# One decoder layer on one core: the dispatch step of the experts stage in another order, with work moved between engines, and merged weight loads

## The chip, the cores and the metric

One core of one Trainium2 chip runs the whole program in one launch. A core has TensorE (PE in the rows), VectorE (DVE), ScalarE (ACT), GpSimd (POOL) and SyncE (SP, here only an issuer of DMAs). The metric is the device time in microseconds (us), lower is better.

## The reference

The input `x` is 128 sequences of 64 tokens of 128 numbers. Three residual blocks follow one another:

```
x = x + attn(layernorm(x))            # 128 positions attend per token column: softmax(tanh(q k)), values are the input
x = x + xattn(layernorm(x), ctx)      # 16 heads of 8
x = x + ffn(layernorm(x))             # soft mixture of 16 experts with 16 slots each
# ffn, for each sequence b of 64 tokens n, with xn = layernorm(x)*gamma + beta
logits   = (xn/|xn| * scale) @ (mu/|mu|)           # n x 256 slots
dispatch = softmax(logits over n); combine = softmax(logits over the 256 slots)
slot_in  = dispatch^T @ xn                         # 256 slots x 128
slot_out = gelu(slot_in @ w1 + b1) @ w2 + b2       # per expert, hidden 32
out      = combine @ slot_out
```

## The kernel before

The program is hand-written per engine: each engine has its own stream of instructions, in the order in which it stands in the code, and semaphores between them. There are four parts, one after the other. All are loops over 16 chunks of 512 tokens, software-pipelined: in step `t` an engine works on chunk `t` in one phase, on chunk `t+1` in an earlier phase, and so on.

1. `self_attention` (first 93 us). SP first issues eight chunks of `x`, then the list `loads` (36 DMAs of weights, L174), four context chunks (L177), and only then goes on with one more chunk of `x` (L171) and one result chunk `x1` out (L181) per step. DVE normalises each chunk (`xn`, L233, four pieces of 128x128 of a chunk), ACT makes `yT`, `xT`, `th`, `pr`. `x1` has two buffers, so the `x1` of chunk 2 (L253) waits until that of chunk 0 has landed in DRAM.
2. `cross_attention`, which the change leaves alone.
3. `experts_in`, the dispatch part. For a chunk: statistics (DVE L1013, L1035), the power -0.5 of the variance (POOL, four ops ending with L956), normalised tokens `hat` (DVE L1025), `xn` = gamma and beta (POOL L963, L965), squares `junk` (ACT L1097), their sum and clamp (DVE L1008, L1019), the power -0.5 of it and times `scale` (POOL `rn`, L941, L943), unit tokens `xu` (DVE L1047), transposed `xuT` (PE L1161, ACT L1077), the logits in both layouts, transposed (PE L1125, called lT here) and not (PE L1131, lA). From them maxima `cm` and `rm` (DVE L1000, L1003), which PE turns into rows (L1140, L1141, here mT), ACT negates (`neg`, L1066), and PE adds back onto the logits as a shift by products with 0/1 matrices `pick` and `sel` (L1149, L1153). ACT takes the exponentials `comb` (L1071) and `disp` (L1083). In the next step PE gathers `slot_in` in two halves (L1115, here g0 and g1), both through the same two PSUM banks, so that g1 waits until ACT has copied the half of g0 (`e_slot_in`, L1057); then come the hidden layer (L1169), the sums of `disp` (L1177) and their copy `raw` (ACT L1091). The sums go through DRAM (SP L915 to L927, with waits in between) to the reciprocal `inv` (DVE L1041) and back to `rden`, and POOL makes `scaled` and `hidden` from them (L981, L984).
4. `experts_out`, which runs in the same block behind it: second layer and combination (PE L1286, L1300), with `comb` of each chunk loaded back from DRAM (SP L1206).

## Time and profile before

| what | us |
|---|---|
| median of 3 runs (lowest, highest) | 626.12 (625.14, 627.65) |
| the profiled execution, and its span | 625.29, 623.5 |
| self attention, 0 to 93.18: PE busy, DVE busy | 64.19, 58.36 |
| cross attention, 93.18 to 326.64: PE busy, DVE busy | 210.57, 179.21 |
| dispatch, start, 326.64 to 371.50: PE, POOL | 20.34, 31.31 |
| dispatch, 13 equal steps, 371.50 to 504.51: PE, POOL | 123.60, 88.47 |
| dispatch, end, 504.51 to 536.93: PE | 21.02 |
| experts out, 536.93 to 623.50: PE | 80.33 |

The kernel's time is 1.8 us more than the span, which runs from the first to the last recorded instruction. Where the PE is busy for all but some per cent of a stretch, the question is what its order of work costs; where it is not, who it waits for. A row of the timeline names the start, the duration, the engine and line, the operation with output and inputs, how many were merged into the row, and in square brackets how long the engine was idle before it and who ended that.

### The profile page before, as it was taken

To read this page: it belongs to the slowest core of one execution; us is meant where nothing else is said; L and a number is where in the kernel's file an instruction comes from. 1 tells how busy PE (TensorE), PEld (TensorE's weight loads), DVE (VectorE), ACT (ScalarE), POOL (GpSimd) and SP (SyncE) were. 2 spreads that over 40 slices of the span, in tenths; PEclk is the share of its full clock that TensorE was granted. 3 is DMA by queue.
4 is the path that set the end of the run, shared out by engine and by line. 5 is a ranking of instruction groups with operands and counts; after the bars stand their busy time and mean duration, and the time that the engine had idled before them with its cause. 6 is when DMAs were issued, how large, how long until landed. Compare 5 with 4: busy or idle time off the path is not lost. (4 is left out here: it accounts for less than half of the span.)

```text
span 623.5 us, 19720 instructions
## 1 busy us (share of the span) xinstructions
PE 520.1 (83%) x7660; PEld 371.6 (60%) x7660; DVE 410.1 (66%) x1187; ACT 345.1 (55%) x487; POOL 286.9 (46%) x369
## 2 busy tenths in 40 slices
PE   4748867989889999999860599999999983999996
PEld 3536655555356666666640355655555552999995
...
GB/s 181 87 178 120 76 58 129 165 137 44 2 22 38 26 36 39 31 30 40 38 20 1 0 70 54 90 68 88 72 100 59 103 56 71 132 152 150 150 149 100
DMA packets 60912, 49.30 MB, mean 79 GB/s; under 512 B 15648, under 2 KB 50592, under 8 KB 60832
## 3 DMA queue, kind: packets, MB, share of 16 engines
...
## 5 line engine op out<-in xcount | busy, mean ns | idle before, releaser
L567 DVE TENSOR_REDUCE c_mx<-ps 128x16 f32<-128x1024 f32 x64 | 78.0, 1218 | 12.9 <-PE ps L722 12.9
L521 POOL TENSOR_TENSOR c_k_bd<-c_k,w_mask 128x512 bf16<-128x512 f32 x80 | 83.7, 1071 | 1.2 <-DVE c_work L605 1.2
L1286 PE MATMUL ps<-w_w,h_bd 128*64 128x128 f32 x1024 | 71.5, 279 | 6.3 <-DVE o_slot_out L1238 6.3
L644 ACT ACTIVATE c_work<-ps 128x2048 f32<-128x2048 f32 x32 | 60.0, 1874 | 26.8 <-PE ps L751 26.8
L1286 PEld LDWEIGHTS ps<-w_w,h_bd 128*64 128x64 f32 x1024 | 63.2, 141 | 7.2 <-DVE o_slot_out L1238 7.2
L1230 ACT ACTIVATE h_bd<-hidden 32x512 f32 (+1 forms) x64 | 40.2, 628 | 41.4 <-PE ps L1286 40.8
L1057 ACT ACTIVATE e_slot_in<-ps 128x1024 f32<-128x1024 f32 x32 | 32.8, 1024 | 51.8 <-PE ps L1115 51.8
L1262 DVE TENSOR_TENSOR o_slot_out<-ps,w_b 128x512 f32<-128x512 f32 x64 | 44.0, 687 | 20.7 <-PE ps L1286 20.3
L1000 DVE TENSOR_REDUCE e_cm<-ps 128x16 f32<-128x1024 f32 x16 | 19.6, 1225 | 49.8 <-PE ps L1125 49.8
L1115 PE MATMUL ps<-e_disp,e_xn 64*128 64x256 f32 x256 | 36.3, 400 | 9.5 <-ACT e_slot_in L1057 8.3
L654 ACT ACTIVATE c_q_bd<-x_all,w_mask 128x512 f32<-128x512 f32 x64 | 42.8, 719 | 0.0
L1300 PE MATMUL ps<-o_slot_out,ctx_sb 128*64 128x129 f32 x512 | 41.9, 274 | 1.0 <-DMA ctx_sb<-combine_scratch 1.0
L1125 PE MATMUL ps<-e_xuT,w_mu 128*128 128x512 f32 x64 | 34.8, 669 | 4.5 <-ACT e_xuT L1077 4.5
L541 POOL COPY c_v_bd<-c_v 64x512 f32<-64x512 f32 x32 | 21.8, 681 | 35.8 <-PE ps L771 27.2
L751 PE MATMUL ps<-c_q_bd,c_k 32*64 32x256 f32 x1024 | 35.5, 375 | 0.4 <-issue 0.4
L771 PE MATMUL ps<-c_work,c_v_bd 128*18 128x64 f32 x2048 | 35.7, 223 | 0.0
L981 POOL TENSOR_TENSOR e_scaled<-e_raw,e_rden 128x512 f32<-128x512 f32 x16 | 20.3, 1270 | 32.3 <-DMA e_rden<-dispatch_inverses 32.3
L1115 PEld LDWEIGHTS ps<-e_disp,e_xn 64*128 64x128 f32 x256 | 23.3, 186 | 19.9 <-issue 19.3
L941 POOL TENSOR_TENSOR e_rn<-e_sq,w_neg_half 128x4 f32<-128x4 f32 x16 | 16.7, 1041 | 39.2 <-DVE e_sq L1019 39.1
L771 PEld LDWEIGHTS ps<-c_work,c_v_bd 128*18 128x18 f32 x2048 | 30.0, 99 | 7.5 <-issue 7.5
L1300 PEld LDWEIGHTS ps<-o_slot_out,ctx_sb 128*64 128x64 f32 x512 | 33.2, 137 | 1.5 <-DMA ctx_sb<-combine_scratch 1.5
L1097 ACT ACTIVATE e_junk<-e_xn 128x512 f32<-128x512 f32 x16 | 10.1, 630 | 43.1 <-POOL e_xn L965 43.1
...
## 6 DMA issues: line engine op xcount, KB each, us to landing
x_all<-x_scratch SPq DMA_DIRECT2D x128, 64.0 KB, 2.3
...
```

What stands on the lines that cost most here:

```text
L521: ins = nc.gpsimd.tensor_tensor(k_bd[:, c.m2, s, :], k32[:, c.v, :], w["mask8"][:, s:s + 1].to_broadcast([P, TOK]), ALU.mult)
L567: nc.vector.reduce_max(mx[:, c.m2, :, p], ps[:, SCORE:SCORE + 2, :].rearrange("p a (h m) -> p (a h) m", m=N), AX_X).then_inc(mx_sb.sem, 1)
L644: nc.scalar.activation(prob[:, h, :], ps[:, 0:4, :].rearrange("p a b -> p (a b)"), ACT.Exp, scale=float(HD) ** -0.5).then_inc(p_sb.sem, 1)
L654: ins = nc.scalar.activation(q_bd[:, c.m2, j, :], q32[:, c.v, :], ACT.Copy, scale=w["mask4"][:, j:j + 1])
L751: ins = nc.tensor.matmul(ps[N * r:N * (r + 1), T, a * 4 * N:(a + 1) * 4 * N].rearrange("p (j n) -> p j n", j=4), k32[rows, c.v, k_at:k_at ...
L771: ins = nc.tensor.matmul(ps[32 * j:32 * j + 2 * V1, VALUE, to:to + N], v_bd[:, c.m2, 2 * u + a, 4 * T + j, :], prob[:, u, of:of + N], star ...
L1115: ins = nc.tensor.matmul(ps[:, 6 + r, a * ES:(a + 1) * ES], xn[at, c.m4, 2 * h + a, :], disp[at, c.m2, 2 * h + a, :], start=True, stop=True)
L1125: ins = nc.tensor.matmul(ps[:, 3 + h, :], w["mu"][:, h * P:(h + 1) * P], xuT[:, c.m2, :], start=True, stop=False, skip_group_check=True)
L1230: ins = nc.scalar.activation(h_bd[at, c.m2, :, :, e, :].rearrange("p s g k -> p g s k"), hidden[at, :, bass.ts(c.v, SC * SLOTS)].rearrange ...
L1262: nc.vector.tensor_tensor(slot_out[:, c.m2, 2 * p:2 * p + 2, :, 0:D], ps[:, p, :].rearrange("p (s a d) -> p s a d", s=2, a=2), w["b2"][:]. ...
L1286: ins = nc.tensor.matmul(ps[64 * (g % 2):64 * (g % 2) + 64, p, at:at + D], h_bd[:, c.m2, s % 2 * PC + s // 2, g].rearrange("p e k -> p (e ...
L1300: ins = nc.tensor.matmul(ps[N * r:N * (r + 1), 4 + p // 2, (p % 2) * (D + 1):(p % 2 + 1) * (D + 1)], comb[:, c.m2, h, s * N:(s + 1) * N], ...
```

## The change

Self attention: of the four pieces of `xn` of a chunk DVE makes two and ACT the other two, as `Identity` with a per-partition scale and a per-partition bias `shift` = -mean times the root; POOL makes `shift` with two more small ops. Loads: `w2` comes in one DMA (before: four), `b2` in eight (before: sixteen), so 25 in place of 36. Dispatch part: `hat` is made by ACT in four pieces in the same way (POOL makes its `shift` with two more small ops), `neg` by DVE, the two powers of -0.5 are one POOL op over eight columns, the factor `scale` is folded into `mu` once, `xu` is one DVE op. The maxima and the identity that turns them are bf16; mT writes them to four groups of partitions (0, 32, 64, 96), and `pick` and `sel` stand in those groups, so that the products of the shift go to different row tiles of PE. The memsets of `sel32` and `pick32` and their affine selects are gone; `pick` and `sel` are made by DVE from the identity. The phases move: `scaled` and `hidden` one step later, `xn` by one step later relative to `hat`, and PE's order within a step is another.

PE, one steady step of `experts_in`, before (L1125 lT, L1131 lA, L1115 the gathers, L1140 and L1141 mT, L1149 and L1153 the shift, L1161 the transposes of `xu`):

```order
L1125 MATMUL ps<-e_xuT,w_mu 128x512 x2
L1131 MATMUL ps<-w_mu,e_xuT 128x256 x4
L1115 MATMUL ps<-e_disp,e_xn 128x256 x4
L1140 MATMUL ps<-w_ident,e_cm 8x128 x2
L1141 MATMUL ps<-w_ident,e_rm 8x128
L1115 MATMUL ps<-e_disp,e_xn 128x256 x4
L1149 MATMUL ps<-e_neg,e_pick 128x128 x8
L1153 MATMUL ps<-e_neg,e_sel 128x256 x4
L1161 MATMUL ps<-w_ident,e_xu 128x128 x4
L1169 MATMUL ps<-e_slot_in,w_w 32x128 x16
L1177 MATMUL ps<-e_disp,w_ones 32x256 x8
```

The same step now, up to the hidden layer, whose two rows stay as they were:

```order
L1164 MATMUL ps<-e_xuT,w_mu 128x512 x2
L1153 MATMUL ps<-e_disp,e_xn 128x256 x4
L1172 MATMUL ps<-w_mu,e_xuT 128x256 x4
L1153 MATMUL ps<-e_disp,e_xn 128x256 x4
L1182 MATMUL ps<-e_ident,e_cm 8x128 x4
L1185 MATMUL ps<-e_ident,e_rm 8x128 x2
L1192 MATMUL ps<-w_ident,e_xu 128x128 x4
L1200 MATMUL ps<-e_neg,e_pick 128x128 x2
L1204 MATMUL ps<-e_neg,e_sel 128x256
L1200 MATMUL ps<-e_neg,e_pick 128x128 x2
L1204 MATMUL ps<-e_neg,e_sel 128x256
```

The gather g0 has moved ahead of lA, so that lA stands between the two gathers; mT comes after g1; the transposes of `xu` have moved between mT and the shift; and the shift is interleaved (the last two rows come twice more).

ACT, one steady step of `experts_in`, before:

```order
L1057 ACTIVATE e_slot_in<-ps 128x2x2x256
L1066 ACTIVATE e_neg<-ps 8x384
L1057 ACTIVATE e_slot_in<-ps 128x2x2x256
L1071 ACTIVATE e_comb<-ps 128x1024
L1077 ACTIVATE e_xuT<-ps 128x512
L1083 ACTIVATE e_disp<-ps 128x1024
L1091 ACTIVATE e_raw<-ps 128x1024
L1097 ACTIVATE e_junk<-e_xn 128x512
```

And now:

```order
L1100 ACTIVATE e_hat<-x_all,e_shift,e_inv_root 128x128 x4
L1091 ACTIVATE e_slot_in<-ps 128x2x2x256
L1108 ACTIVATE e_junk<-e_xn 128x512
L1091 ACTIVATE e_slot_in<-ps 128x2x2x256
L1114 ACTIVATE e_xuT<-ps 128x512
L1119 ACTIVATE e_comb<-ps 128x1024
L1126 ACTIVATE e_disp<-ps 128x1024
L1134 ACTIVATE e_raw<-ps 128x1024
```

The `neg` has gone and four pieces of `hat` have come in at the head of the step; `junk` stands between the two slot copies, and `xuT` ahead of `comb`.

SP, the end of the list of loads in `self_attention`, before and now:

```order
L174 DMA w_w<-in_L_ffn_w 128x128
L174 DMA w_b<-in_L_ffn_b 128x1
L174 DMA w_w<-in_L_ffn_w 128x128
L174 DMA w_b<-in_L_ffn_b 16x128 x16
L177 DMA ctx_sb<-in_ctx 128x4x128 x4
```

```order
L176 DMA w_b<-in_L_ffn_b 128x1 x4
L176 DMA w_w<-in_L_ffn_w 128x4x128
L176 DMA w_b<-in_L_ffn_b 16x2x128 x8
L179 DMA ctx_sb<-in_ctx 128x4x128 x4
```

Eleven DMAs fewer stand ahead of the context chunks, and behind those come the result chunks.

```diff
+                    if c.plus(-2): pool.wait_ge(normed_act.sem, normed_act.at(c.plus(-2)))
                     nc.gpsimd.tensor_tensor(rstd[:, c.m2, :], mv[:, c.m2, :, 1], w["ln_eps"][:], ALU.add).then_inc(rooted.sem, 1)
-                    pool.wait_ge(rooted.sem, rooted.at(c, 1))
+                    nc.gpsimd.tensor_tensor(shift[:, c.m2, :], mv[:, c.m2, :, 0], neg_one[:], ALU.mult).then_inc(rooted.sem, 1)
+                    pool.wait_ge(rooted.sem, rooted.at(c, 2))
                     nc.gpsimd.tensor_tensor(rstd[:, c.m2, :], rstd[:, c.m2, :], w["neg_half"][:, 0:BC],
                                             ALU.pow).then_inc(rooted.sem, 1)
+                    pool.wait_ge(rooted.sem, rooted.at(c, 3))
+                    nc.gpsimd.tensor_tensor(shift[:, c.m2, :], shift[:, c.m2, :], rstd[:, c.m2, :], ALU.mult).then_inc(rooted.sem, 1)
...
-                    for b in range(BC):
+                    for b in range(BC // 2):
                         ins = nc.vector.tensor_scalar(xn[:, c.m4, b, 0:D], xc[:, b, :], mv[:, c.m2, b, 0:1],
                                                       rstd[:, c.m2, b:b + 1], ALU.subtract, ALU.mult)
...
+                c = t.plus(2)
+                if c:
+                    act.wait_ge(rooted.sem, rooted.at(c))
+                    if c.plus(-4): act.wait_ge(o_ps.sem, o_ps.at(c.plus(-4)))
+                    for b in range(BC // 2, BC):
+                        ins = nc.scalar.activation(xn[:, c.m4, b, 0:D], x_sb[:, bass.ds(c.v * BC + b, 1), :].rearrange("p a d -> p (a d)"),
+                                                   ACT.Identity, bias=shift[:, c.m2, b:b + 1], scale=rstd[:, c.m2, b:b + 1])
+                    ins.then_inc(normed_act.sem, 1)
...
+                    pe.wait_ge(normed_act.sem, normed_act.at(c))
...
-        loads.append((w["w2"][:, g, :], a["L0_ffn_w2"][4 * g:4 * g + 4].rearrange("c h d -> (c h) d")))
-    for e in range(EXPERTS):
-        loads.append((w["b2"][SLOTS * (e % 8):SLOTS * (e % 8 + 1), e // 8, :],
-                      a["L0_ffn_b2"][e:e + 1, :].to_broadcast([SLOTS, D])))
+    loads.append((w["w2"][:], a["L0_ffn_w2"].rearrange("(g c) h d -> (c h) g d", g=4)))
+    for e in range(8):
+        loads.append((w["b2"][SLOTS * e:SLOTS * (e + 1), :, :],
+                      a["L0_ffn_b2"].rearrange("(a e) d -> e a d", a=2)[e:e + 1].to_broadcast([SLOTS, 2, D])))
...
         for t in steps:
             c = t.plus(3)
             if c:
-                pool.wait_ge(clamped.sem, clamped.at(c))
-                if c.plus(-2): pool.wait_ge(xu_sb.sem, xu_sb.at(c.plus(-2)))
-                nc.gpsimd.tensor_tensor(rn[:, c.m2], sq[:, c.m2], w["neg_half"][:, 0:PC], ALU.pow).then_inc(unit.sem, 1)
-                pool.wait_ge(unit.sem, unit.at(c, 1))
-                nc.gpsimd.tensor_tensor(rn[:, c.m2], rn[:, c.m2], w["scale"][:].to_broadcast([P, PC]),
-                                        ALU.mult).then_inc(unit.sem, 1)
-            c = t.plus(5)
+                pool.wait_ge(hat_sb.sem, hat_sb.at(c))
...
+                nc.gpsimd.tensor_tensor(xn[:, c.m4], hat[:, c.m2], spread(w["gamma"][:]), ALU.mult).then_inc(normed.sem, 1)
...
+                nc.gpsimd.tensor_tensor(xn[:, c.m4], xn[:, c.m4], spread(w["beta"][:]), ALU.add).then_inc(normed.sem, 1)
+            c = t.plus(-3)
...
+            c, u = t.plus(5), t.plus(3)
...
                 nc.gpsimd.tensor_tensor(rc, rc, v, ALU.add).then_inc(root.sem, 1)
                 pool.wait_ge(root.sem, root.at(c, 3))
-                nc.gpsimd.tensor_tensor(rc, rc, w["neg_half"][:], ALU.pow).then_inc(root.sem, 1)
...
+            if u: pool.wait_ge(clamped.sem, clamped.at(u))
+            if c and u:
+                nc.gpsimd.tensor_tensor(inv_root[:, c.m2], inv_root[:, c.m2], halves[:], ALU.pow).then_inc(root.sem, 1)
+                pool.wait_ge(root.sem, root.at(c, 4))
+            elif c:
+                nc.gpsimd.tensor_tensor(rs[:, c.m2], rs[:, c.m2], halves[:, 1], ALU.pow).then_inc(root.sem, 1)
+                pool.wait_ge(root.sem, root.at(c, 4))
+            elif u:
+                nc.gpsimd.tensor_tensor(rn[:, u.m2], rn[:, u.m2], halves[:, 0], ALU.pow).then_inc(unit.sem, 1)
+            if c:
+                nc.gpsimd.tensor_tensor(shift[:, c.m2], mv[:, c.m2, :, 0], rs[:, c.m2], ALU.mult).then_inc(root.sem, 1)
+                pool.wait_ge(root.sem, root.at(c, 5))
+                nc.gpsimd.tensor_tensor(shift[:, c.m2], shift[:, c.m2], minus[:], ALU.mult).then_inc(root.sem, 1)
             if t.k == -4:
                 nc.gpsimd.memset(rm[:], 0.0).then_inc(cleared, 1)
...
                 nc.gpsimd.memset(h_bd[:], 0.0).then_inc(cleared, 1)
...
+            c = t.plus(2)
+            if c:
+                unit_wait(dve, c)
+                if c.plus(-2): dve.wait_ge(xuT_ps.sem, xuT_ps.at(c.plus(-2)))
+                nc.vector.tensor_tensor(xu[:, c.m2], xn[:, c.m4], rn[:, c.m2].rearrange("p (q o) -> p q o", o=1).to_broadcast([P, PC, D]),
+                                        ALU.mult).then_inc(xu_sb.sem, 1)
...
-                nc.vector.reduce_max(rm[:, c.m2, 0:PC], ps[:, 1:3, :].rearrange("p a (b e) -> p (a b) e", e=ES), AX_X).then_inc(max_sb.sem, 1)
+            c = t.plus(1)
+            if c:
+                for h in range(2):
+                    dve.wait_ge(lA_ps.sem, lA_ps.at(c, h + 1))
+                    nc.vector.reduce_max(rm[:, c.m2, 2 * h:2 * h + 2], ps[:, 1 + h, :].rearrange("p (b e) -> p b e", e=ES),
+                                         AX_X).then_inc(max_sb.sem, 1)
...
+                dve.wait_ge(mT_ps.sem, mT_ps.at(c))
+                if c.plus(-2): dve.wait_ge(shA_ps.sem, shA_ps.at(c.plus(-2)))
+                nc.vector.tensor_scalar(neg[:, c.m2], ps[:, 5, 0:ES], -1.0, None, ALU.mult).then_inc(neg_sb.sem, 1)
...
+            c = t.plus(4)
+            if c:
+                act.wait_ge(root.sem, root.at(c))
+                if c.plus(-2): act.wait_ge(normed.sem, normed.at(c.plus(-2), 1))
+                for p in range(PC):
+                    ins = nc.scalar.activation(hat[:, c.m2, p], tok(c, p), ACT.Identity, bias=shift[:, c.m2, p:p + 1],
+                                               scale=rs[:, c.m2, p:p + 1])
+                ins.then_inc(hat_sb.sem, 1)
             slots(t.plus(0), 0)
+            c = t.plus(3)
+            if c:
+                act.wait_ge(normed.sem, normed.at(c))
+                if c.plus(-2): act.wait_ge(summed.sem, summed.at(c.plus(-2)))
+                nc.scalar.activation(junk[:, c.m2], xn[:, c.m4], ACT.Square).then_inc(squared.sem, 1)
+            slots(t.plus(0), 1)
...
-                act.wait_ge(mT_ps.sem, mT_ps.at(c))
-                if c.plus(-2): act.wait_ge(shA_ps.sem, shA_ps.at(c.plus(-2)))
-                nc.scalar.activation(neg[:, c.m2], ps[0:SC, 5, 0:ES + P], ACT.Copy, scale=-1.0).then_inc(neg_sb.sem, 1)
...
+            gather(t.plus(0), 0)
+            if c:
...
+                    if p % 2: ins.then_inc(lA_ps.sem, 1)
+            gather(t.plus(0), 1)
+            if c:
...
-                    nc.tensor.transpose(ps[0:SC, 5, h * P:(h + 1) * P], cm[:, c.m2, h, :], w["ident"][:])
-                nc.tensor.transpose(ps[0:SC, 5, 2 * P:3 * P], rm[:, c.m2, :], w["ident"][:]).then_inc(mT_ps.sem, 1)
...
-                for h in range(2):
-                    for p in range(PC):
-                        ins = nc.tensor.matmul(ps[:, 3 + h, p * P:(p + 1) * P], pick[:, p, :], neg[0:PC, c.m2, ES:ES + P],
-                                               start=False, stop=True, skip_group_check=True)
-                ins.then_inc(shT_ps.sem, 1)
-                for p in range(PC):
-                    ins = nc.tensor.matmul(ps[:, 1 + p // 2, p % 2 * ES:(p % 2 + 1) * ES], sel[:, p, :], neg[:, c.m2, 0:ES],
-                                           start=False, stop=True, skip_group_check=True)
-                ins.then_inc(shA_ps.sem, 1)
+                    for g in range(2):
+                        nc.tensor.matmul(ps[64 + 32 * g:64 + 32 * g + SC, 5, h * P:(h + 1) * P], cm[:, c.m2, h, :], ident[:],
+                                         start=True, stop=True)
+                for g in range(2):
+                    ins = nc.tensor.matmul(ps[32 * g:32 * g + SC, 5, 0:P], rm[:, c.m2, :], ident[:], start=True, stop=True)
+                ins.then_inc(mT_ps.sem, 1)
...
+            c = t.plus(1)
+            if c:
+                pe.wait_ge(neg_sb.sem, neg_sb.at(c))
+                for p in range(PC):
+                    for h in range(2):
+                        rows = slice(32 * h, 32 * h + SC)
+                        ins = nc.tensor.matmul(ps[:, 3 + h, p * P:(p + 1) * P], pick[rows, p, :], neg[rows, c.m2, 0:P],
+                                               start=False, stop=True, skip_group_check=True)
+                    if p == PC - 1: ins.then_inc(shT_ps.sem, 1)
+                    rows, q = slice(64 + 32 * (p % 2), 64 + 32 * (p % 2) + SC), p % 2 * 2 + p // 2
+                    ins = nc.tensor.matmul(ps[:, 1 + q // 2, q % 2 * ES:(q % 2 + 1) * ES], sel[rows, q, :], neg[rows, c.m2, 0:ES],
+                                           start=False, stop=True, skip_group_check=True)
+                ins.then_inc(shA_ps.sem, 1)
```

(`unit_wait` waits for the power that covers `rn` of that chunk; `w["mu"]` is now made with the factor `scale`.)

## Rows read from the trace of the kernel before

**Rows 1.** Busy time by engine (x instructions), granted clock, DMA; thirteen steps.
```profile
371.50:504.51 133.01, 123.60 (x1244) 77.71 (x1236) 78.04 (x235) 80.97 (x104) 88.47 (x112) 1.00 0.24 79
```

**Rows 2.** Timeline, PE, one step of the dispatch part.
```profile
422.66 1.98 PE L1125 MATMUL ps<-e_xuT,w_mu 128*128 128x512 f32 x4
424.48 1.89 PE L1131 MATMUL ps<-w_mu,e_xuT 128*128 128x256 f32 x8
426.30 1.14 PE L1115 MATMUL ps<-e_disp,e_xn 64*128 64x256 f32 x8
427.69 0.38 PE L1140 MATMUL ps<-w_ident,e_cm 128*8 128x128 f32 x2 [0.25 <-DVE e_rm L1003]
...
428.65 1.14 PE L1115 MATMUL ps<-e_disp,e_xn 64*128 64x256 f32 x8 [0.47 <-ACT e_slot_in L1057]
429.71 0.62 PE L1149 MATMUL ps<-e_neg,e_pick 4*128 4x128 bf16 x8
...
430.70 0.66 PE L1161 MATMUL ps<-w_ident,e_xu 128*128 128x128 f32 x4
431.28 1.08 PE L1169 MATMUL ps<-e_slot_in,w_w 128*32 128x128 f32 x32
432.30 0.66 PE L1177 MATMUL ps<-e_disp,w_ones 64*32 64x256 f32 x16
```

**Rows 3.** Timeline, ACT and POOL, the same step.
```profile
428.40 0.46 ACT L1066 ACTIVATE e_neg<-ps 8x384 bf16<-8x384 f32 x1
...
429.15 1.04 POOL L941 TENSOR_TENSOR e_rn<-e_sq,w_neg_half 128x4 f32<-128x4 f32 x1 [2.09 <-DVE e_sq L1019]
...
430.27 0.20 POOL L943 TENSOR_TENSOR e_rn<-e_rn,w_scale 128x4 f32<-128x4 f32 x1
...
433.06 1.02 ACT L1091 ACTIVATE e_raw<-ps 128x1024 f32<-128x1024 f32 x1
```

**Rows 4.** Timeline, self attention, SP (issue time of a DMA) and DVE.
```profile
20.06 7.37 SPq L174 DMA_DIRECT2D w_b<-in_L_ffn_b  x16
...
30.65 0.38 SPq L181 DMA_DIRECT2D x_scratch<-a_x  x1
...
35.86 1.13 DVE L253 SCALAR_TENSOR_TENSOR a_x<-ps,a_rden,x_sb 128x128 f32<-128x128 f32 x4 [10.12 <-DMA x_scratch<-a_x]
```

**Rows 5.** Timeline, self attention, a steady step.
```profile
65.79 0.63 ACT L299 ACTIVATE a_pr<-a_th 128x512 f32<-128x512 f32 x1
...
67.47 0.60 PE L334 MATMUL ps<-w_ident,a_xn 128*128 128x128 f32 x4
```

**Rows 6.** Timeline, the start of the dispatch part.
```profile
335.71 0.12 POOL L967 MEMSET e_rm<- 128x16 f32 x1
...
338.10 3.50 POOL L976 MEMSET h_bd<- 128x4096 f32 x1
...
348.89 3.78 PE L1125 MATMUL ps<-e_xuT,w_mu 128*128 128x512 f32 x4 [3.79 <-ACT e_xuT L1077]
```

**Rows 7.** Timeline, the end of the dispatch part.
```profile
512.59 1.02 ACT L1071 ACTIVATE e_comb<-ps 128x1024 f32<-128x1024 f32 x1
...
536.93 0.67 PE L1300 MATMUL ps<-o_slot_out,ctx_sb 128*64 128x129 f32 x8 [0.64 <-DMA ctx_sb<-combine_scratch]
```

**Rows 8.** Timeline, SP and DVE, the way of the sums in one step.
```profile
431.78 0.36 SPq L911 DMA_DIRECT2D combine_scratch<-e_comb  x1
...
439.85 0.34 SPq L927 DMA_DIRECT2D e_sums<-dispatch_sums  x1
...
441.44 0.25 DVE L1041 RECIPROCAL e_inv<-e_sums 128x16 f32<-128x16 f32 x1 [0.83 <-DMA e_sums<-dispatch_sums]
```

**Rows 9.** Timeline, ACT, the nearest operations to the new pieces.
```profile
90.17 0.28 ACT L303 ACTIVATE w_wqT<-ps 128x128 f32<-128x128 f32 x1 [5.00 <-PE ps L352]
...
115.95 0.69 ACT L684 ACTIVATE x_all<-ps,w_bqk 128x512 f32<-128x512 f32 x1 [0.58 <-PE ps L816]
```

**Rows 10.** Timeline, POOL, a power over two columns.
```profile
89.45 0.70 POOL L205 TENSOR_TENSOR raw_norm<-raw_norm,w_half 128x2 f32<-128x2 f32 x1 [12.92 <-DVE raw_norm L265]
```

More of the change, by code:

```diff
@@ L899, in experts_in, with unit_wait @@
     comb_out = kit.pairs("e_comb_out")
-    steps = [Chunk(None, t) for t in range(-5, CHUNKS + 2)]
+    steps = [Chunk(None, t) for t in range(-5, CHUNKS + 3)]
     def tok(c, p):
         return x_all[:, c.v * PC + p, :]
+    def unit_wait(eng, c):
+        if c.plus(2): eng.wait_ge(root.sem, root.at(c.plus(2), 4))
+        else: eng.wait_ge(unit.sem, c.v - (CHUNKS - 2) + 1)
     @block.sync
```

168 lines of the change are left out of this document (71 added, 97 removed).

## The prediction

> **What bounds the kernel now.** I read the windows by stage first, then the timeline of the stages that the change touches, and the chain of waits to see which engine it runs on. The cross attention (233 us) and the last part (87 us) are not touched. The dispatch part has thirteen steps of equal length, 133.01/13 = 10.23 us, in which PE is busy for 93% at full clock, DVE for 59%, ACT for 61% and POOL for 67% [rows 1]. So PE's order of work is the clock there. Its step, from start to start [rows 2]: lT 1.82, lA 1.82, from g0 to g1 2.35, g1 1.06, shift (L1149 and L1153) 0.99, transposes 0.58, hidden layer 1.02, and the sums take what is left of 10.23, 0.59. A gather itself takes 1.06 (g1 to the shift); so 2.35 - 1.06 = 1.29 of the step are the way g0, ACT's slot copy, g1, in whose shadow lies mT (three products, the first two 0.38). The row of L1140 shows PE waiting for DVE's `rm`, that of g1 for ACT.
>
> The other engines have slack. POOL was idle 2.09 before `rn` [rows 3], so its work fills 8.14 of a step. ACT ends `raw` at 434.08, 1.19 after the next step began at 422.66 + 10.23 = 432.89, and has nothing urgent until g0 is done. SP's way from the issue of `comb` to that of the last DMA is 8.4 us in the step shown, and then 1.6 us to landing, for which DVE waits 0.83 [rows 8].
>
> Self attention has one hole: DVE waits 10.12 us, from 25.7 to 35.86, until the first `x1` has landed, because SP issues it at 30.65 only, after the weights and the context; it then takes 5.2 us [rows 4]. In its steady steps the loop goes through PE and ACT's `th` and `pr`, not through DVE's `xn` [rows 5].
>
> **The change, part by part.**
>
> *Loads.* Sixteen `b2` DMAs take SP 7.37 us, 0.46 each [rows 4]. Eleven fewer: 5.1 us. The context chunks and the result chunks are issued that much earlier, and the hole of 10.12 shrinks to 5.0. It could shrink by nothing if the landing were bound by bytes that start when they did; but the issue order, not the load on the queues, sets when the burst begins. It could be 6.6 if PE also comes out of the shorter hole at the higher clock. I take 5.1.
>
> *Normalisation split in self attention.* DVE sheds two pieces, ACT gains two. A 128x128 ACT copy takes 0.28, and a bias operand makes 0.69 out of about 0.63 for 128x512 [rows 5, 9], so a piece with bias and scale is between 0.28 and 0.40, two of them at most 0.8. `pr` ends at 66.42 and the transposes that need the pieces start at 67.47, 1.05 later [rows 5]. Cover 0.25, cost nothing; if the cover were gone, some 0.2 on each of 14 steps, 3 us. POOL's two extra small ops (0.20 each, as L943 [rows 3]) come a step ahead. DVE gives nothing back, since it isn't in the loop.
>
> *PE's step in the dispatch part.* lA now stands between the gathers: 1.82 of work over a way of 1.29, so the wait is gone, and mT comes out of the shadow. What stays is 1.82 + 1.06 + 1.82 + 1.06 + 0.58 + 1.02 + 0.59 = 7.95. mT is six bf16 products of 128 columns. Eight such `pick` products and four of 256 take 0.99, or about 0.06 for 128 columns: 0.35 in line, 0.17 if pairs in different column groups run side by side, 0.5 if it is as dear as today's three products. I take 0.35, since each product also loads weights. The shift: same number of columns, spread over four row groups. Upper bound 0.99, in line as now. Lower bound: the gathers are row-tiled in two; lA streams the same columns in 1.82 untiled, half is 0.91, and they take 1.06, so 0.15 are lost; 0.99/4 + 0.15 = 0.40. I take 0.55, near the tiled end, because the gathers show that row groups do overlap here. Last, 0.10 for the handovers: `neg` (0.46 on ACT [rows 3], and two handovers) against transposes of 0.58 that cover most of it, and steps in which SP's way is the long one. Step: 7.95 + 0.35 + 0.55 + 0.10 = 8.95, between 8.5 and 9.5. Saved 1.28 a step, 16.6 us over thirteen.
>
> The new order goes from whole-array products to column groups, back, to four row groups, and to column groups again. No row has the price of such a change of tiling by itself; the 0.15 that a gather loses [rows 2] bounds it. If each of three such changes cost 0.15 on top, a step would be 9.4 long; that is part of rival 1. The Trainium skill (page TensorEngine Tiling (Array Packing), Key Properties) speaks for it: a change of tiling mode, unlike a change of tile, drains TensorE. By that rule the whole would come out near 606, by the rows near 599.5.
>
> *ACT.* `neg` (0.46) goes, four pieces of `hat` come, 1.1 to 1.6. They stand behind `raw`: 1.19 + 1.6 = 2.8 into the step, and g0 ends at 2.88. Covered, and g1 would forgive another 0.6, as it waits for lA. ACT's total is 80.97/13 = 6.2, and about 1.1 more, under 8.95.
>
> *POOL.* It loses `rn` (1.04) and its scale (0.20), gains two small ops, and its other power is over eight columns. Two columns took 0.70 [rows 10] and four 1.04, 0.17 a column, so eight are 1.72, or 2.1 if it is proportional. 8.14 - 1.24 + 0.40 + 0.68 is 8.0, at most 8.4. Still under 8.95, but the next in line.  DVE loses `hat`, gains `neg`; `xu` in one op.
>
> *The start.* POOL's fills and selects between 335.71 and 338.10 go, 2.4; the memset of `h_bd` (3.50) [rows 6] still delays the first tokens, now directly. Against it stand DVE's new memsets, about 0.3, and four small ops for two chunks, with their handovers about 1.0, and the merged power takes off about 0.4. First logits 1.5 earlier (between 0.5 and 2.5). The two steps from 348.89 to 371.50 save at least what the later ones do, 2.6.
>
> *The end.* From `comb` of the last chunk (over at 513.61) everything hangs on SP's serial DMAs up to the loaded `comb` at 536.93 [rows 7], which don't change. But `comb` now ends at 1.82 + 1.06 + 1.82 + 1.06 + 0.35 + 0.58 + 0.55 + 0.04 + 1.02 = 8.30 into its step, before 513.61 - 504.51 = 9.10: 0.8.
>
> Sum: 5.1 + 1.5 + 2.6 + 16.6 + 0.8 = 26.6. The profiled execution took 625.29, so 598.7; its median is 0.8 higher: **599.5 us**.
>
> **The rivals.**
>
> 1. *The tiled shift doesn't pay*: row groups don't overlap for such short products, or changes of tiling take back what the overlap gives. For it: each product is only 128 or 256 columns. Against: the gathers, which are tiled and lose 0.15 in all. Step 9.4; fifteen steps at 0.45 more, 6.7: 606.
> 2. *POOL, or DVE behind it, becomes the clock*, because the eight-column power is dearer or because POOL's and DVE's accesses collide. It needs 1 us more than worked out. Step 9.4: 606.
> 3. *The hole in self attention stays*, as the landing is bound by bytes: 599.5 + 5.1 = 604.6.
> 4. *Slower: SP's way becomes the clock.* SP starts a step at `comb` and must be through before the next; DVE waits for its last DMA, in order, ahead of `xu`, statistics and maxima, which makes a loop over two steps: 8.3 to the end of `comb`, SP's way, 1.6 landing, 1.9 for DVE, against two steps and the 1.9 at which DVE needs lT. With the 8.4 of [rows 8] a step could not be under (8.3 + 8.4 + 1.6 + 1.9 - 1.9)/2 = 9.15; steps before and after it are shorter, so I count it in the 0.10. It makes the kernel slower once a step is over 10.23 + (5.1 + 1.5 + 0.8 + 3.1)/15 = 10.93, so with SP's way over 10.9. With 12 us: 625.3 - 7.4 + 15 x 1.77 = 644, 645 beside the median. For it: the same bytes in shorter steps. Against: DMA engines are busy for 24% [rows 1].
>
> **How the numbers follow.** Forecast 0.58, rival 1 0.15, rival 2 0.11, rival 3 0.08, rival 4 0.06, and 0.02 that gains and losses cancel. Within the forecast the step of 8.5 gives 7 us less, so 592.5, and with the clock gained 591. The range from 592 to 608 takes in the forecast's bounds, rivals 1 to 3, and leaves out rival 4, two of rivals 1 to 3 together, and the lucky end. A difference of 0.5%, 3.1 us, is what a measurement of this kernel can tell from none. Faster 0.91, same 0.03, slower 0.06.
>
> **What would show it.** Self attention: DVE's wait before the `x1` op of chunk 2 near 5 us, and PE's steady step as long as before. Dispatch: starts of lT 8.95 apart (8.5 to 9.5); no wait of PE for `rm` nor for the slot copy; shift 0.4 to 0.6 from first product to hidden layer; POOL idle for about 1 in a step. The power over eight columns 1.7. Last part as it was, 86.6. What would make it wrong: PE waiting for `neg`, for `xuT` or for `raw` in each step, or DVE standing long before `inv`.

## The result, and the profile after

The changed kernel takes **596.87 us** (median of four runs, 592.56 to 598.50) against 625.63 (623.68 to 627.65) before: ratio 0.953, 95% interval 0.947 to 0.959. The forecast was 599.5 in a range of 592 to 608. The profiled execution is the fastest of the four, 592.56 with a span of 590.8; before it was 625.29 with a span of 623.5. So the stages below (us) add up to 32.7, while the medians lie 28.8 apart; no profile shows where the 3.9 between them lie.

| part | before | after | gain | forecast |
|---|---|---|---|---|
| self attention | 93.18 | 86.92 | 6.26 | 5.1 |
| cross attention (not touched) | 233.46 | 231.70 | 1.76 | 0 |
| from its end to the first lT | 22.25 | 20.70 | 1.55 | 1.5 |
| first two steps | 22.61 | 18.37 | 4.24 | 2.6 |
| thirteen steps | 133.01 | 113.94 | 19.07 | 16.6 |
| lT of the last chunk to the end of its `comb` | 9.10 | 8.26 | 0.84 | 0.8 |
| from there to the first combination product | 23.32 | 24.07 | -0.75 | 0 |
| experts out | 86.57 | 86.85 | -0.28 | 0 |

The windows view of the changed kernel over the thirteen steps, which answers to [rows 1]: PE, PEld, DVE, ACT and POOL busy, granted clock, DMA share, GB/s.

```profile
357.69:471.63 113.94, 113.94 (x1283) 67.95 (x1275) 73.34 (x182) 93.20 (x135) 92.49 (x113) 1.00 0.27 92
```

A step is 113.94/13 = 8.76 us, and PE is busy in all of it, where it was busy for 93%. ACT went from 61% to 82% and POOL from 67% to 81%. POOL's shares are too low, since some of its records are missing (113 of 130 instructions here, 112 of 130 before): in a step with all ten of them POOL is busy for 7.87 of 8.76 us, 90%:

```profile
409.18:417.94 8.76, 8.76 (x110) 5.22 (x102) 5.80 (x16) 7.46 (x12) 7.87 (x10) 1.00 0.27 95
```

One step on PE in the timeline of the changed kernel, which answers to [rows 2]:

```profile
427.80 1.98 PE L1164 MATMUL ps<-e_xuT,w_mu 128*128 128x512 f32 x4
429.72 1.13 PE L1153 MATMUL ps<-e_disp,e_xn 64*128 64x256 f32 x8
430.78 1.99 PE L1172 MATMUL ps<-w_mu,e_xuT 128*128 128x256 f32 x8
432.71 1.13 PE L1153 MATMUL ps<-e_disp,e_xn 64*128 64x256 f32 x8
433.77 0.22 PE L1182 MATMUL ps<-e_ident,e_cm 128*8 128x128 bf16 x2
...
433.98 0.66 PE L1192 MATMUL ps<-w_ident,e_xu 128*128 128x128 f32 x4
434.59 0.23 PE L1200 MATMUL ps<-e_neg,e_pick 8*128 8x128 bf16 x2
...
434.77 0.22 PE L1200 MATMUL ps<-e_neg,e_pick 8*128 8x128 bf16 x2
...
434.96 1.08 PE L1213 MATMUL ps<-e_slot_in,w_w 128*32 128x128 f32 x32
435.98 0.66 PE L1221 MATMUL ps<-e_disp,w_ones 64*32 64x256 f32 x16
436.57 1.98 PE L1164 MATMUL ps<-e_xuT,w_mu 128*128 128x512 f32 x4
```

None of these rows carries a wait. By start to start: lT 1.92, g0 1.06, lA 1.93, g1 1.06, mT 0.21, transposes 0.61, shift 0.37, hidden layer 1.02, sums 0.59. POOL, DVE and ACT in the same step, which answers to [rows 3]:

```profile
426.71 1.65 POOL L1001 TENSOR_TENSOR e_inv_root<-e_inv_root,e_halves 128x8 f32<-128x8 f32 x1 [0.42 <-DVE e_inv_root L1077]
...
428.39 0.69 DVE L1033 TENSOR_TENSOR e_xu<-e_xn,e_inv_root 128x512 f32<-128x512 f32 x1 [0.51 <-POOL e_inv_root L1001]
428.44 0.71 POOL L1009 TENSOR_TENSOR e_shift<-e_mv,e_inv_root 128x4 f32<-128x4 f32 x1
...
429.45 1.66 ACT L1100 ACTIVATE e_hat<-x_all,e_shift,e_inv_root 128x128 f32<-128x128 f32 x4
...
436.59 0.25 DVE L1082 RECIPROCAL e_inv<-e_sums 128x16 f32<-128x16 f32 x1 [1.26 <-DMA e_sums<-dispatch_sums]
```

The power over eight columns takes 1.65, and POOL's only wait that a row shows is 0.42 in a step of 8.76, beside gaps of under 0.1 between its operations: it is next in line. The four pieces of `hat` take ACT 1.66. `inv` waits 1.26 for SP's DMA, but what `xu` waits for is POOL's power.

Self attention, SP's issues and DVE's wait, which answers to [rows 4]:

```profile
17.78 3.82 SPq L176 DMA_DIRECT2D w_b<-in_L_ffn_b  x8
...
24.83 0.38 SPq L183 DMA_DIRECT2D x_scratch<-a_x  x1
...
30.03 1.12 DVE L261 SCALAR_TENSOR_TENSOR a_x<-ps,a_rden,x_sb 128x128 f32<-128x128 f32 x4 [5.21 <-DMA x_scratch<-a_x]
```

The first `x1` is issued at 24.83 instead of 30.65, and the hole is 5.21 instead of 10.12. In a steady step ([rows 5]) nothing moved: `pr` starts 3.83 after `pr`, and ACT's two pieces of `xn` lie under PE's product with `pr`, whose next work starts 1.05 after `pr` has ended, as before:

```profile
59.47 0.63 ACT L318 ACTIVATE a_pr<-a_th 128x512 f32<-128x512 f32 x1
60.00 0.87 ACT L299 ACTIVATE a_xn<-x_sb,a_shift,a_rstd 128x128 f32<-128x128 f32 x2
...
61.15 0.60 PE L354 MATMUL ps<-w_ident,a_xn 128*128 128x128 f32 x4
...
63.30 0.63 ACT L318 ACTIVATE a_pr<-a_th 128x512 f32<-128x512 f32 x1
```

At the start of the dispatch part the memset stands on POOL ahead of the first tokens, and the first lT, at half clock, comes at 339.32, which answers to [rows 6]:

```profile
325.04 3.53 POOL L1014 MEMSET h_bd<- 128x4096 f32 x1
...
339.32 3.78 PE L1164 MATMUL ps<-e_xuT,w_mu 128*128 128x512 f32 x4 [2.86 <-ACT e_xuT L1114]
```

### The profile page after: what moved, and what is told of

It reads as the page before. It is cut to its first block and busy times, and to the rows that moved or that the text cites. A ratio compares the mean times of both kernels' runs of the same rounds, so it can differ in the third digit from the quotient of the medians.

```text
span 590.8 us, 19858 instructions
## 1 busy us (share of the span) xinstructions
PE 505.0 (85%) x7708; PEld 357.8 (61%) x7708; DVE 389.9 (66%) x1081; ACT 376.9 (64%) x567; POOL 293.8 (50%) x399
## 5 line engine op out<-in xcount | busy, mean ns | idle before, releaser
L587 DVE TENSOR_REDUCE c_mx<-ps 128x16 f32<-128x1024 f32 x64 | 78.0, 1219 | 14.2 <-PE ps L742 13.3
L1274 ACT ACTIVATE h_bd<-hidden 32x512 f32 (+1 forms) x64 | 40.3, 629 | 41.1 <-PE ps L1330 40.5
L561 POOL COPY c_v_bd<-c_v 64x512 f32<-64x512 f32 x32 | 21.8, 682 | 35.4 <-PE ps L791 26.8
L1153 PE MATMUL ps<-e_disp,e_xn 64*128 64x256 f32 x256 | 37.2, 410 | 2.6 <-ACT e_raw L1134 1.4
L1164 PE MATMUL ps<-e_xuT,w_mu 128*128 128x512 f32 x64 | 33.5, 648 | 4.2 <-ACT e_xuT L1114 2.9
L1100 ACT ACTIVATE e_hat<-x_all,e_shift,e_inv_root 128x128 f32<-128x128 f32 x64 | 26.5, 485 | 16.1 <-POOL e_shift L1011 15.3
L1153 PEld LDWEIGHTS ps<-e_disp,e_xn 64*128 64x128 f32 x256 | 22.7, 189 | 21.2 <-issue 19.8
L1172 PE MATMUL ps<-w_mu,e_xuT 128*128 128x256 f32 x128 | 32.5, 398 | 0.0
L1052 DVE TENSOR_REDUCE e_rm<-ps 128x2 bf16<-128x512 f32 x32 | 22.1, 692 | 15.4 <-PE ps L1172 15.4
```

The costliest lines, as they stand in the source:

```text
L587: nc.vector.reduce_max(mx[:, c.m2, :, p], ps[:, SCORE:SCORE + 2, :].rearrange("p a (h m) -> p (a h) m", m=N), AX_X).then_inc(mx_sb.sem, 1)
L1153: ins = nc.tensor.matmul(ps[:, 6 + r, a * ES:(a + 1) * ES], xn[at, c.m4, 2 * h + a, :], disp[at, c.m2, 2 * h + a, :], start=True, stop=True)
L1164: ins = nc.tensor.matmul(ps[:, 3 + h, :], w["mu"][:, h * P:(h + 1) * P], xuT[:, c.m2, :], start=True, stop=False, skip_group_check=True)
L1172: ins = nc.tensor.matmul(ps[:, 1 + p // 2, p % 2 * ES:(p % 2 + 1) * ES], xuT[:, c.m2, p * P:(p + 1) * P], w["mu"][:], start=p % 2 == 0, st ...
L1274: ins = nc.scalar.activation(h_bd[at, c.m2, :, :, e, :].rearrange("p s g k -> p g s k"), hidden[at, :, bass.ts(c.v, SC * SLOTS)].rearrange ...
```

## The experiments

Each was timed in turns with the kernel before on the same chip; its median there was 625.5, 625.2, 626.6 or 624.9. "Ratio" is to it. The changed kernel itself lies at 596.87, with single runs up to 4.3 below that, so a difference to it under about 3 us is not read from the times but from the traces.

### Loads: in the kernel before alone, and undone in the changed one

```diff
-        loads.append((w["w2"][:, g, :], a["L0_ffn_w2"][4 * g:4 * g + 4].rearrange("c h d -> (c h) d")))
-    for e in range(EXPERTS):
...
+    loads.append((w["w2"][:], a["L0_ffn_w2"].rearrange("(g c) h d -> (c h) g d", g=4)))
+    for e in range(8):
...
```

This edit made to the kernel before, and nothing else:

> The kernel before with the eleven DMAs fewer and nothing else. Theory (the hole in self attention is set by the order of issues on SP): DVE's wait in front of the x1 op of chunk 2 falls from 10.1 to about 5 us, the kernel is 5 to 6 us faster than before, everything behind it unchanged. Rival (the landing is bound by bytes in the queues): the wait stays near 10 and the time stays within 1 us.

The reverse edit made to the changed kernel (36 loads again):

> The changed kernel with the 36 loads of before. Theory (parts add up): self attention is 5 to 6 us longer than in the changed kernel, about 92 us, and the rest is the same, so about 602 us. Rival (the split of xn between DVE and ACT shortens self attention by itself): self attention is clearly shorter than 92 us, by 1 us or more.

Measured: 621.23 (ratio 0.992, interval 0.989 to 0.995), 4.3 less than before; and 600.61 (ratio 0.962, 0.958 to 0.966), 3.7 more than the changed kernel. DVE's wait before the same operation, first in the kernel before with the merged loads, then in the changed kernel with the 36 loads:

```profile
30.66 1.13 DVE L253 SCALAR_TENSOR_TENSOR a_x<-ps,a_rden,x_sb 128x128 f32<-128x128 f32 x4 [5.22 <-DMA x_scratch<-a_x]
```

```profile
35.37 1.13 DVE L261 SCALAR_TENSOR_TENSOR a_x<-ps,a_rden,x_sb 128x128 f32<-128x128 f32 x4 [9.56 <-DMA x_scratch<-a_x]
```

The hole follows the list of loads, 4.3 to 4.9 us, in either kernel, so rival 3 falls: the hole is set by when SP gets to the result chunks. The times moved by less than the 5 to 6 us that I expected.

### `xn` of self attention on DVE alone

```diff
-                    for b in range(BC // 2):
+                    for b in range(BC):
...
-                    for b in range(BC // 2, BC):
-                        ins = nc.scalar.activation(xn[:, c.m4, b, 0:D], x_sb[:, bass.ds(c.v * BC + b, 1), :].rearrange("p a d -> p (a d)"),
-                                                   ACT.Identity, bias=shift[:, c.m2, b:b + 1], scale=rstd[:, c.m2, b:b + 1])
...
```

> The changed kernel with all four pieces of xn in self attention on DVE again (the small ops for the shift stay on POOL). Theory (the steady loop goes through PE and ACT, DVE has cover): steady steps of 3.84 us as before and after, no more than 0.5 us lost in all, at the restart behind the hole. Rival (the split brought the 1.3 us of self attention that the loads don't explain): self attention 1 us or more longer, by 0.1 us in each step.

Measured: 594.41 (ratio 0.950, 0.948 to 0.953), not different from the changed kernel. In the trace `pr` of the last chunk starts at 80.65 instead of 78.23, 2.4 later where I had expected at most 0.5, but from chunk 4 on both need the same time (42.4 and 42.1). So in the steady step the split is worth nothing. `pr` of chunk 0 starts 1.2 later (16.21, not 15.00), and 0.5 more is the hole, which varies between runs (3.9 to 5.7 in all kernels with merged loads). Not all of the 1.2 is the split: this run keeps the two small ops for `shift` on POOL, and DVE's first `xn` waits for them. In the kernel before with merged loads, which has neither, `pr` of chunk 0 starts at 15.63, so that about 0.6 is left for the split.

### The order of PE: lA ahead of both gathers, and the order alone in the kernel before

```diff
-            gather(t.plus(0), 0)
-            if c:
...
                     if p % 2: ins.then_inc(lA_ps.sem, 1)
+            gather(t.plus(0), 0)
             gather(t.plus(0), 1)
```

> The changed kernel with lA directly behind lT again, both gathers behind it, the rest of the new order kept (mT behind g1). Theory: PE waits for ACT's slot copy between the gathers, 1.2 us with its handovers, and saves about 0.2 because lT and lA are one stretch without a change of tiling (3.64 together as before, 3.85 when apart); step 8.76 + 1.0 = 9.7 to 9.9, the kernel 14 to 17 us slower than the changed one. Rival (the order of the gathers is worth little, as ACT would be late in another place): step under 9.3.

Measured: 611.24 (ratio 0.977, 0.975 to 0.980), 14.4 over the changed kernel. PE in its timeline:

```profile
442.30 1.13 PE L1153 MATMUL ps<-e_disp,e_xn 64*128 64x256 f32 x8
...
444.64 1.13 PE L1153 MATMUL ps<-e_disp,e_xn 64*128 64x256 f32 x8 [1.22 <-ACT e_slot_in L1091]
```

From g0 to g1 it is 2.34 again, as before (2.35), and the step is 9.84, 1.08 longer than 8.76: 1.28 of waiting is back, and lT and lA take 3.65 instead of 3.85. So with everything else of the change in place, this one place is worth 14 of the 19 us. But the same order put into the kernel before, with everything else as it was:

```diff
             slots(t.plus(0), 0)
+            slots(t.plus(0), 1)
...
-            slots(t.plus(0), 1)
...
+            gather(t.plus(0), 0)
+            if c:
...
-            gather(t.plus(0), 0)
+            gather(t.plus(0), 1)
...
-            gather(t.plus(0), 1)
```

On ACT both slot copies now stand ahead of `neg`; on PE the order is lT, g0, lA, g1, mT, transposes of `xu`, shift.

> The kernel before with only the new order: on PE lT, g0, lA, g1, mT, transposes, shift; on ACT both slot copies ahead of neg. neg stays on ACT, the shift in line, hat on DVE, 36 loads. Theory (the order needs neg on DVE): neg queues behind the second slot copy, so PE waits for it about 0.5 us in front of the shift; with mT 0.5 out of the shadow and the shift 0.99 the step is 10.0 to 10.2, and the kernel within 4 us of before. Rival (the order brings its gain of 0.8 us a step alone): step 9.3 to 9.5, 12 us faster than before.

Measured: 625.59 (ratio 1.000, 0.998 to 1.002); the expectation held. Its steps are 10.13 and 10.33 long in turns. PE and ACT in its timeline:

```profile
438.24 1.03 ACT L1057 ACTIVATE e_slot_in<-ps 128x1024 f32<-128x1024 f32 x1 [1.31 <-PE ps L1115]
...
438.55 0.60 PE L1149 MATMUL ps<-w_ident,e_xu 128*128 128x128 f32 x4
439.17 0.46 ACT L1067 ACTIVATE e_neg<-ps 8x384 bf16<-8x384 f32 x1
...
439.69 0.61 PE L1157 MATMUL ps<-e_neg,e_pick 4*128 4x128 bf16 x8 [0.54 <-ACT e_neg L1067]
```

ACT can't begin `neg` before the slot copy of g1 is done (439.2), and PE stands 0.54 before the shift, which is still 0.98 long. Of the 1.28 that lA fills, 0.33 go to mT, out of its shadow, 0.2 to lT and lA, which take longer apart, and 0.54 to `neg`; the rest is a late slot copy (ACT begins the one of g0 at 435.92, 0.94 after g0, behind `junk`, and PE waits 0.17 for it before g1). So the order alone, with this order on ACT, gains nothing; it pays with the rest of the change. Which parts of the rest it needs is shown only for the shift, in the next experiment. The same order with `neg` ahead of the second slot copy on ACT was not run. An estimate for it: in [rows 2] and [rows 3] `neg` starts 0.71 after mT's first row, so here it could be over at about 439.4 instead of 439.6, which gives some 0.2 back in each step, 3 to 4 us in all.

### The shift in one row tile for each kind

```diff
-                        rows = slice(32 * h, 32 * h + SC)
...
+                for h in range(2):
+                    for p in range(PC):
+                        ins = nc.tensor.matmul(ps[:, 3 + h, p * P:(p + 1) * P], pick[0:SC, p, :], neg[0:SC, c.m2, 0:P],
...
-                    rows, q = slice(64 + 32 * (p % 2), 64 + 32 * (p % 2) + SC), p % 2 * 2 + p // 2
...
+                for q in range(PC):
+                    ins = nc.tensor.matmul(ps[:, 1 + q // 2, q % 2 * ES:(q % 2 + 1) * ES], sel[64:64 + SC, q, :], neg[64:64 + SC, c.m2, 0:ES],
...
```

> The changed kernel with the shift's products in line: the eight with pick all in the row group at partition 0, then the four with sel all in that at 64. Same number of products and columns. Theory (row groups run side by side, the shift took 0.37 us from first start to the hidden layer): now about 0.9 to 1.0, the step 9.3 to 9.4 in place of 8.76, the kernel 8 to 9 us slower than the changed one, about 605 us. Rival (the shift was hidden behind another wait): step under 8.9, under 2 us slower.

Measured: 602.12 (ratio 0.963, 0.961 to 0.966), 5.3 over the changed kernel, less than the 8 to 9 that I expected. The shift runs from 439.62 to the hidden layer at 440.40, and the step is 9.17:

```profile
439.62 0.45 PE L1199 MATMUL ps<-e_neg,e_pick 8*128 8x128 bf16 x5
...
440.09 0.38 PE L1203 MATMUL ps<-e_neg,e_sel 8*128 8x256 bf16 x2
...
440.40 1.08 PE L1212 MATMUL ps<-e_slot_in,w_w 128*32 128x128 f32 x32
```

0.78 instead of 0.37, and 0.41 is just what the step grows by. Four row groups in turns pay, and rival 1 falls; and at 9.17 most of the new order's gain is still there, so it doesn't hang on a shift of 0.37. (The two kinds still stand in different groups here, so 0.78 is not yet the 0.99 of [rows 2].)

### Two powers on POOL

```diff
-                nc.gpsimd.tensor_tensor(inv_root[:, c.m2], inv_root[:, c.m2], halves[:], ALU.pow).then_inc(root.sem, 1)
+                nc.gpsimd.tensor_tensor(rs[:, c.m2], rs[:, c.m2], halves[:, 1], ALU.pow)
+                nc.gpsimd.tensor_tensor(rn[:, c.m2], rn[:, c.m2], halves[:, 0], ALU.pow).then_inc(root.sem, 1)
```

> The changed kernel with the two powers of -0.5 as two POOL ops over four columns each (about 1.04 each, against 1.65 for the one over eight). POOL is idle 0.4 us in a step of the changed kernel. Theory (POOL is next in line with 0.4 us in hand): 0.4 more work just fits, step 8.8 to 8.9, the kernel at most 2 us slower. Rival (the chain clamp, power, xu, maxima is what sets the step): step 9.1 or more, 5 us slower.

Measured: 596.01 (ratio 0.953, 0.951 to 0.956), the step 8.77; the expectation held. POOL in its timeline:

```profile
437.32 1.02 POOL L1001 TENSOR_TENSOR e_inv_root<-e_inv_root,e_halves 128x4 f32<-128x4 f32 x1
...
438.31 1.01 POOL L1002 TENSOR_TENSOR e_inv_root<-e_inv_root,e_halves 128x4 f32<-128x4 f32 x1
...
446.10 1.02 POOL L1001 TENSOR_TENSOR e_inv_root<-e_inv_root,e_halves 128x4 f32<-128x4 f32 x1
```

The merged power saves 0.4, as two take 2.0, but without it only POOL's idle time is used up: from power to power no row of POOL shows a wait in 8.78, exactly at the edge. The merge is worth nothing yet, and any more on POOL would show.

### `hat` on DVE, ahead of the maxima, and then behind the clamp

```diff
+            c = t.plus(4)
+            if c:
+                dve.wait_ge(root.sem, root.at(c, 4))
...
+                for p in range(PC):
+                    ins = nc.vector.tensor_scalar(hat[:, c.m2, p], tok(c, p), mv[:, c.m2, p, 0:1], rs[:, c.m2, p:p + 1],
+                                                  ALU.subtract, ALU.mult)
...
```

This stands on DVE between the statistics and `cm`, and ACT's four pieces go.

> The changed kernel with hat in the dispatch part on DVE again, four pieces between the statistics and the maxima; the shift is still computed on POOL. Theory (PE is the clock and DVE has room: its maxima would end about 1 us later and still ahead of the end of g1): step 8.8 to 9.0, the kernel less than 3 us slower; moving hat to ACT is no gain by itself. Rival (DVE can't take it): PE waits for rm, step 9.3 or more, 8 us slower.

Measured: **628.5** (ratio 1.005, 1.003 to 1.007). My expectation was wrong by 30 us; its rival had the wait right, PE for `rm`, but at 8 us. In its timeline:

```profile
434.45 1.27 POOL L975 TENSOR_TENSOR e_xn<-e_hat,w_gamma 128x512 f32<-128x512 f32 x1
434.86 4.63 DVE L1046 TENSOR_SCALAR e_hat<-x_all,e_mv,e_inv_root 128x128 f32<-128x128 f32 x4
435.80 1.26 POOL L977 TENSOR_TENSOR e_xn<-e_xn,w_beta 128x512 f32<-128x512 f32 x1
437.02 1.27 POOL L982 TENSOR_TENSOR e_scaled<-e_raw,e_rden 128x512 f32<-128x512 f32 x1
438.37 1.04 POOL L985 TENSOR_TENSOR hidden<-e_scaled,w_b 128x512 f32<-128x512 f32 x1
439.41 1.21 DVE L1054 TENSOR_REDUCE e_cm<-ps 128x16 bf16<-128x1024 f32 x1
```

Four pieces take 4.63, one for each of POOL's four operations: they end at 435.80, 437.15, 438.37 and 439.49, each 0.08 or 0.09 after one of those (435.72, 437.06, 438.29, 439.41). POOL is not slowed. `cm` starts 3.2 after lT has ended (434.32 + 1.92), and through `neg`, the clamp and POOL's power this is a closed loop over DVE and POOL, with steps of 8.8 to 13.3 and PE waiting for `rm`. Part of the loss is the clock: in the step before the one shown PE had waited 3.00 for `rm`, and its hidden layer then took 1.94 instead of 1.08, with the granted clock at 0.50 from 431.5 to 433.3. To see whether the pieces are slow everywhere on DVE, the same four went behind the clamp, where POOL runs its power:

> The changed kernel with hat made by DVE again, as in the experiment that put it there ahead of the maxima, but now behind the clamp at the end of DVE's step, where POOL runs its power and DVE otherwise waits for it. Theory A (beside POOL's multiplications and additions of 128x512 a piece of hat takes DVE 1.16 us, as four took 4.63 there, while in the kernel before four took 1.11 beside POOL's power; and what is slow stood ahead of the maxima): the four pieces take 1.0 to 1.4 us, they fit DVE's idle 1.6 us behind the clamp, the step stays 8.77 and the time is 593 to 599, ratio 0.947 to 0.958. Theory B (a piece of hat is slow in the changed kernel wherever it stands, or ACT is needed for it): the four pieces take over 4 us, xu comes 3 us late, the step is 10 us or more and the time is over 612. Theory C (only the place ahead of the maxima hurt, not the pieces' length): pieces of over 1 us each here too, yet a step under 9.2.

Measured: 594.64 (ratio 0.953, 0.949 to 0.957), theory A. DVE and POOL in its timeline:

```profile
437.40 1.11 DVE L1083 TENSOR_SCALAR e_hat<-x_all,e_mv,e_inv_root 128x128 f32<-128x128 f32 x4
437.63 1.65 POOL L1001 TENSOR_TENSOR e_inv_root<-e_inv_root,e_halves 128x8 f32<-128x8 f32 x1 [0.42 <-DVE e_inv_root L1077]
438.74 0.25 DVE L1090 RECIPROCAL e_inv<-e_sums 128x16 f32<-128x16 f32 x1 [0.22 <-DMA e_sums<-dispatch_sums]
```

The same instructions take 1.11, the step is 8.76. ACT was not needed for `hat`; a place beside POOL's power was. The rule on the page SBUF — State Buffer of the Trainium skill (Who interferes with whom) fits the slow pieces: DVE and GpSimd share a pair of ports as an exclusive lock, which a DVE operation needs in a mode with two ports, or with two inputs in SBUF while GpSimd reads SBUF, and the loser blocks. That these pieces run in such a mode no run shows. And by the same rule POOL's power, which reads and writes SBUF, should have held up the pieces that start during it; here it didn't (1.11 for four, beside a power of 1.65), so for the power the measurement decides against the rule.

### The memset of `h_bd` behind everything

```diff
             if t.k == -4:
                 nc.gpsimd.memset(rm[:], 0.0).then_inc(cleared, 1)
+            if t.k == CHUNKS:
                 nc.gpsimd.memset(h_bd[:], 0.0).then_inc(cleared, 1)
```

> The changed kernel with the memset of h_bd moved from the start of the dispatch part to the end of its second last chunk. In the chain that ended last of the changed kernel this memset stands with 3.45 us in front of the first xn. Theory: the first logits come 3.5 us earlier, and as every later stage follows from them the kernel is 3 to 3.5 us faster, about 593 us where the changed one has 596.9. Rival (the first xn would wait for hat on ACT, or the memset blocks DVE and POOL at the end): less than 1.5 us.

Measured: 593.36 (ratio 0.948, 0.944 to 0.951). The first lT starts at 336.01 instead of 339.32, from a cross attention that ended at the same time, but the third at 357.77, as in the changed kernel (357.69). The windows of the changed kernel, and then of this one, show where the 3.3 us went:

```profile
340.00:344.00 4.00, 4.00 (x7) 1.91 (x6) 2.27 (x6) 1.41 (x4) 3.76 (x5) 0.50 0.00 0
344.00:348.00 4.00, 2.74 (x28) 1.71 (x27) 3.29 (x10) 1.59 (x4) 1.72 (x4) 0.95 0.00 0
348.00:352.00 4.00, 3.05 (x13) 1.47 (x13) 2.23 (x6) 2.90 (x5) 3.75 (x4) 1.00 0.33 131
```

```profile
340.00:344.00 4.00, 3.12 (x16) 2.25 (x15) 2.92 (x8) 1.56 (x4) 1.95 (x3) 0.75 0.00 0
344.00:348.00 4.00, 2.66 (x19) 1.29 (x18) 2.14 (x7) 2.44 (x4) 3.01 (x6) 0.67 0.30 122
348.00:352.00 4.00, 4.00 (x12) 1.67 (x11) 1.62 (x4) 1.73 (x5) 2.44 (x2) 0.50 0.02 9
```

The granted clock is 0.50 (1.2 GHz) in 348 to 352 where it was 1.00 (2.4 GHz). It had been there: in a view cut into half microseconds it rises at 342.0, falls again after 345 and rises once more at 352.2, so that lT of the second step takes 3.75 instead of 1.95. In the changed kernel it rises after 344 and stays. PE's idle times in the first step are the same in both, 0.88 and 1.34, so they alone don't tell the two apart; why the clock fell here and not there stays open. In the profiled executions the clock took all of the 3.3 us back. The median is 3.5 below, as the expectation had it, but four runs each can't tell that difference from none, and the trace doesn't bear out its way.

### A version from what was found

`xn` on DVE, `hat` on DVE behind the clamp, neither with a `shift` on POOL, the memset late.

> A version made of what the experiments point to: the changed kernel with xn of self attention on DVE alone, hat on DVE behind the clamp, both without their shift on POOL, and the memset of h_bd behind the other work of POOL. POOL has 0.9 us less in each dispatch step, and 3.5 us less in the start. If PE alone sets the step, it stays 8.77 and only the start gains: the way to the first lT is 20.70 - 3.45 - about 2 x 0.9 for two shifts on it = 15 to 16 us. Of this the clock takes back a part, since a start that came 3.3 us sooner in the experiment with the late memset left PE at half its clock until 352 us and ended the first two steps no sooner. Forecast: 590 to 594, ratio 0.943 to 0.950; if the clock takes all of it back, 593 to 597; if the pieces of hat are slow on DVE, over 605.

Measured: **590.52** (six runs, 588.81 to 594.31; ratio 0.947, 0.943 to 0.950), the fastest kernel here, and inside the forecast. Its interval overlaps that of the changed kernel's ratio, so that it is faster than that one is likely, not shown. The first lT starts at 337.13, 17.55 after the last product of cross attention at 319.58 (21.8 in the changed kernel, after 317.54), and this time the clock is at 1.00 in 344 to 352: the first two steps take 18.17, the later ones 8.76. The traces say where it gains: from the start of the last products of cross attention to the third lT it takes 36.9, against 40.5 to 41.9 in the seven others with steps of 8.76 to 9.17, the one with the late memset among them (41.3). From DVE's first memset (320.66) to the first lT it is 16.5, not the 15 to 16 expected. Its timeline shows DVE and POOL in each other's way once more, now with a DVE operation that has two inputs, since `xn` on POOL follows the power at once:

```profile
434.70 1.27 POOL L961 TENSOR_TENSOR e_xn<-e_hat,w_gamma 128x512 f32<-128x512 f32 x1
434.76 1.75 DVE L1014 TENSOR_TENSOR e_xu<-e_xn,e_inv_root 128x512 f32<-128x512 f32 x1 [0.30 <-POOL e_inv_root L987]
436.04 1.61 POOL L963 TENSOR_TENSOR e_xn<-e_xn,w_beta 128x512 f32<-128x512 f32 x1
```

`xu` takes 1.75 instead of 0.69, and POOL's next operation 1.61 instead of 1.27. DVE has the slack for it, so the step doesn't show it.

## Why the prediction was right, by its own steps

**The step of the dispatch part** was forecast at 8.95 and measured 8.76. The mechanism is as put: lA over the way from g0 over the slot copy to g1, PE without a wait; undoing that one place gave back 14 us. The sizes, forecast and measured: the untouched pieces 7.95 and 8.19, mT 0.35 and 0.21, shift 0.55 and 0.37, handovers 0.10 and none. What the step said of changes of tiling, that none has a price in a row, is now filled: lT and lA took 3.64 together and take 3.85 apart (3.65 when put together again), with two changes more, so 0.1 each, if it is the changes, and not the 0.15 of rival 1. That is 0.2 a step, against 0.62 that the interleaved row groups save over [rows 2]. (The Trainium skill's rule in TensorEngine Tiling (Array Packing), Key Properties, that a change of mode drains TensorE, has the right sign, but what it costs here is the smaller of the two.) The 0.55 for the shift, "near the tiled end", was too careful: it came out below even the lower bound of 0.40.

**The loads**: 5.1 forecast, 4.9 in the trace, 4.3 and 3.7 in the two experiments' medians.

**The split in self attention** was costed at nothing in the steady step, rightly, though ACT's two pieces take 0.87, over the bound of 0.8; what it gives is about 0.6 us at the fill of the pipeline, which I had not looked for.

**The start and the first two steps**: 1.55 for 1.5, and 4.24 for 2.6; the latter are at mixed clocks. That 1.55 comes so close is in part luck: from the start of the last products of cross attention to the first lT it took 22.9 in the changed kernel, but 22.1 to 24.0 in the five others with the same start, and 24.5 and 25.4 in the kernel before without and with merged loads. That the memset would stand directly ahead of the first tokens was right, but moving its 3.5 us away, alone, left the third lT where it was.

**ACT and POOL**: 1.66 for `hat` (upper bound 1.6), 1.65 for the power (1.72). "POOL idle for about 1 in a step" was wrong: 0.42, as `shift` takes 0.71 beside `xu`, not 0.20, and the step is shorter. Rival 2 was nearer than its margin of 1 us: 0.4 us more on POOL reaches the edge, as the two powers showed.

**SP's way**, rival 4: the last DMA is issued 6.4 after that of `comb`. The prediction's 8.4 was read with the last DMA's own 0.34 in it, which its 1.6 of landing holds once more: from start to start [rows 8] give 8.1, and the bound on a step is 9.0, not 9.15. DVE's waits for that DMA, 0.2 to 1.8 in the steady steps, lie under POOL's power.

The sum was 26.6 and the stages gave 32.7, of which 1.8 are cross attention. Its length, from first to last product, varied between 230.6 and 233.0 over the kernels here, which all have it alike, and the profiled execution of the changed kernel has the shortest. So the profiled gain is 6.1 over the sum, of which 2.5 are the thirteen steps, 1.6 the first two and 1.2 self attention; the end and the last part lost 1.0. Against the median the forecast is only 2.6 too high. That is the size of what the thirteen steps gave beyond it, but no profile of a median execution shows that the other differences cancel, and that they do is luck as far as the record goes.
